# A gated feed-forward kernel: the transposition of the activations of batches 2 to 7 moves from TensorE to two transposing DMAs per batch

## The reference

```python
scale = cond @ norm_w.T + 1.0                       # (8, 512)
ms = mean(x * x, axis=-1)
h = x * (scale[:, None, :] * rsqrt(ms + 1e-6))
u = h @ up_w.T                                      # up_w: (4096, 512)
val, gate = split(u, 2, axis=-1)
h = val * gelu(gate)                                # exact gelu, 2048 wide
hq = round-to-int8-levels(h), one scale per token   # 127 / max|h|
wq = ternary(down_w), one scale for the matrix
out = hq @ wq.T + x
```

## Time and profile before

| what | value |
|---|---|
| median of the runs | 810.25 us |
| profiled execution: span from first to last instruction | 807.4 us |
| TensorE busy | 772.0 us (96%) |
| DVE busy | 605.6 us (75%) |
| ACT busy | 443.2 us (55%) |
| POOL busy | 255.6 us (32%) |
| DMA queue of SP | 152.06 MB, 55.5% of 16 engines |

### The profile page before, as it was taken

How to read it: one execution, slowest core, us unless ns; L and a number is a source line. 1 busy time by engine, 2 the same in 40 slices (tenths; PEclk the granted TensorE clock), 3 DMA queues, 4 the chain that set the end, 5 groups by cost and what they waited for, 6 DMA issues and landing times.

```text
span 807.4 us, 18034 instructions
## 1 busy us (share of the span) xinstructions
PE 772.0 (96%) x6401; PEld 635.0 (79%) x6401; DVE 605.6 (75%) x852; ACT 443.2 (55%) x1025; POOL 255.6 (32%) x318
## 2 busy tenths in 40 slices
PE   5898988999799999999999999999999999999998
PEld 4687877788688877897788877898788877888753
DVE  5987987799568973899558973898558973887367
ACT  5687767587566643555446643555446643554323
POOL 3875966354422321123212321122212321111021
PEclk9999999999999999999999999999999999999999
DMA  5485764876465554654565554654565545555432
GB/s 207 169 264 170 239 226 175 309 243 218 160 223 198 185 187 148 223 206 145 188 213 200 184 169 151 230 203 140 193 219 195 182 162 162 188 187 175 133 126 83
DMA packets 37963, 152.90 MB, mean 189 GB/s; under 512 B 3608, under 2 KB 4128, under 8 KB 37920
## 3 DMA queue, kind: packets, MB, share of 16 engines
q1 hardware_dynamic: 37376, 152.06, 55.5%
q10 hardware_dynamic: 544, 0.27, 0.1%
HBM read 130.16 MB, written 22.15 MB: 189 GB/s over the span
## 4 chain that ended last, share of the span: by engine, by line
PE 71%; DVE 7%; DMA 1%; issue 1%; ACT 1%; SPq 0%; DVEq 0%; ACTq 0%
PE Y L1142 11%; PE A L1091 11%; PE A L1094 11%; PE A L1093 11%; PE B L1091 8%; PE B L1094 8%; PE B L1093 8%; DVE h L872 2%; DMA wslots<-w_scratch 1%; DVE h L838 1%; PE X L1039 1%; DVE h L832 1%; DVE mpart L851 1%; PE X L1131 1%; DVE q L877 1%
## 5 line engine op out<-in xcount | busy, mean ns | idle before, releaser
L1091 PE MATMUL A<-xT,wslots 128*128 (+1 forms) x1024 | 280.9, 274 | 13.4 <-ACT snapC L616 9.1
L1093 PE MATMUL A<-xT,wslots 128*128 (+1 forms) x1024 | 280.9, 274 | 0.0
L1094 PE MATMUL A<-xT,wslots 128*128 (+1 forms) x1024 | 280.9, 274 | 0.0
L509 POOL TENSOR_TENSOR snapC<-snapC 128x256 f32<-128x256 f32 x128 | 100.5, 785 | 503.4 <-ACT snapC L616 503.3
L1091 PE MATMUL B<-xT,wslots 128*128 (+1 forms) x768 | 210.4, 274 | 2.1 <-DVE h L832 2.1
L1093 PE MATMUL B<-xT,wslots 128*128 (+1 forms) x768 | 210.3, 274 | 0.0
L1094 PE MATMUL B<-xT,wslots 128*128 (+1 forms) x768 | 210.2, 274 | 0.0
L838 DVE SCALAR_TENSOR_TENSOR h<-h,c_all,g 128x512 f32<-128x512 f32 (+1 forms) x128 | 103.7, 810 | 111.0 <-ACT g L639 110.7
L1091 PEld LDWEIGHTS A<-xT,wslots 128*128 128x128 f16 x1024 | 100.7, 98 | 30.3 <-ACT snapC L616 11.0
L1093 PEld LDWEIGHTS A<-xT,wslots 128*128 128x128 f16 x1024 | 100.7, 98 | 14.6
L1094 PEld LDWEIGHTS A<-xT,wslots 128*128 128x128 f16 x1024 | 100.8, 98 | 12.2
(11 more groups left out here) (137 smaller groups left out, 944.0 us busy)
## 6 DMA issues: line engine op xcount, KB each, us to landing
wslots<-w_scratch SPq DMA_DIRECT2D x105, 896.0 KB, 4.6
w_scratch<-wslots SPq DMA_DIRECT2D x15, 896.0 KB, 5.2
wst<-in_L_cond_up_w_dram SPq DMA_DIRECT2D x16, 512.0 KB, 6.5
xin<-in_x_dram SPq DMA_DIRECT2D x8, 1024.0 KB, 7.5
dwb<-in_L_cond_down_w_dram SPq DMA_DIRECT2D x16, 512.0 KB, 4.4
wst<-in_x_dram SPq DMA_DIRECT2D x28, 256.0 KB, 5.3
out_dram<-wst SPq DMA_DIRECT2D x28, 256.0 KB, 2.1
xin<-in_x_dram SPq DMA_DIRECT2D x4, 256.0 KB, 4.1
```

What stands on the lines that cost most here:

```text
L509: pool.tensor_tensor(snapC[:, s % 2, 0:H], snapC[:, s % 2, 0:H], snapC[:, s % 2, H:T], ALU.add)\
L1091: pe.matmul(into, high, xh, start=(start and kp == 0), stop=False, skip_group_check=not start)
L1093: pe.matmul(into, high, xl, start=False, stop=False, skip_group_check=not start)
L1094: mm = pe.matmul(into, low, xh, start=False, stop=last, skip_group_check=not start)
```

## The change

Only x of batches 2 to 7 is touched; batches 0 and 1 keep the old way. The work is done with the tokens on the partitions: DVE multiplies each tile of xin by the token's factor and the channels' scale in one instruction (`normalise_scaled`, two tiles in step 5, two in step 6); for that the scales of all batches are turned once in batch 0 (one transpose, one ACT copy), stored to `scl_rows`, and one row is loaded per batch as a broadcast (`load_scl`). POOL mixes blocks of xin in steps 7 and 10, ACT writes the high parts of one depth pair to a staging buffer `xstage` (in xf's room) in steps 7, 8, 11, 12, DVE the low parts in steps 8, 9, 12, 13, now after `value(s)`. SP then turns the staging buffer, high and low parts together (3584 float16 columns, 128 partitions), into xT by one transposing DMA per depth pair (`turn_x`): the first is issued after the weights of slot 13, the second after those of slot 15, each after a wait of SP for its low parts. ACT's high part of the second pair waits for the first DMA to have landed; TensorE waits for both at the start of the next batch. The 16 transposes of TensorE and the four copies `x_out` of each of these batches go.

```diff
-    RMS_AT, REFINE_AT, NORMALISE_AT = 4, 5, 5
-    XT_AT = {6: 0, 7: 1, 8: 2, 11: 3}
-    XF_AT = {6: 0, 7: 1, 10: 2, 11: 3}
-    XMIX_AT = {8: 0, 12: 1}
-    XHI_AT = {8: 0, 9: 1, 12: 2, 13: 3}
-    XLO_AT = {9: 0, 10: 1, 13: 2, 14: 3}
+    RMS_AT, REFINE_AT = 4, 5
+    NORMALISE_AT = {5: (0, 1), 6: (2, 3)}
+    XMIX_AT = {7: 0, 10: 1}
+    XHI_AT = {7: 0, 8: 1, 11: 2, 12: 3}
+    XLO_AT = {8: 0, 9: 1, 12: 2, 13: 3}
+    XTURN_AFTER = {13: 0, 15: 1}
...
+            def load_scl(b):
+                row = scl_rows[b:b + 1] if isinstance(b, int) else scl_rows[bass.ds(b, 1)]
+                sp.dma_start(scl_b[:, :], row.to_broadcast([P, D])).then_inc(scl_b_loaded, 16)
+
+            def turn_x(b, kp):
+                sp.wait_ge(xlo_ready, 4 * b + (2 * kp + 2))
+                sp.dma_start_transpose(x_turned(b, kp), xstage[:, :, :].rearrange("p a n -> p (a n)"))\
+                  .then_inc(x_turned_in[kp], 16)
...
                 for s in range(5, 15):
                     load_slot(b, s)
+                    if not final and s in XTURN_AFTER:
+                        turn_x(b + 1, XTURN_AFTER[s])
...
                 load_slot(b, 15)
                 if not final:
+                    turn_x(b + 1, XTURN_AFTER[15])
                     load_slot(b + 1, 4)
...
+                    sp.wait_ge(scl_copied, 1)
+                    sp.dma_start(scl_rows.rearrange("b (k p) -> k b p", p=P),
+                                 scl_kb[:, :]).then_inc(scl_stored, 16)
             sp.wait_ge(w_stored[ring_of(3)], 16 * LOADS[ring_of(3)])
+            sp.wait_ge(scl_stored, 16)
+            load_scl(2)
             batch(1, first=True)
...
+            def x_high_stage(b, kp, cut):
+                act.wait_ge(xmix_steps, 8 * b + (4 * kp + (4 if cut else 2)))
+                if cut == 0:
+                    if kp:
+                        act.wait_ge(x_turned_in[0], 16 * (b - 1))
+                    act.activation(xstage[:, 0, 0:4 * H].rearrange("p (h t n) -> p h t n", h=2, n=P), xn_blocks(kp),
+                                   ACT.Copy).then_inc(xhi_ready, 1)
...
+            def normalise_scaled(b, tiles):
+                dve.wait_ge(rstd_ready, b + 1)
+                dve.wait_ge(scl_b_loaded, 16 * (b - 1))
+                for t in tiles:
+                    dve.scalar_tensor_tensor(out=xin[:, t, :], in0=xin[:, t, :], scalar=rstd[:, t:t + 1],
+                                             in1=scl_b[:, :], op0=ALU.mult, op1=ALU.mult).then_inc(xn_ready, 1)
...
-                            normalise(b + 1)
-                        if s in XLO_AT:
-                            x_low(b + 1, *divmod(XLO_AT[s], 2), XLO_AT[s] + 1)
+                        if s in NORMALISE_AT:
+                            normalise_scaled(b + 1, NORMALISE_AT[s])
...
                     value(b, s)
+                    if not final and s in XLO_AT:
+                        x_low_stage(b + 1, *divmod(XLO_AT[s], 2), XLO_AT[s] + 1)
                     largest(of, before)
...
             def batch(b, first=False, final=False):
-                pe.wait_ge(xlo_ready, 4 * b + 4)
+                if first:
+                    pe.wait_ge(xlo_ready, 4 * b + 4)
+                else:
+                    for kp in range(KP):
+                        pe.wait_ge(x_turned_in[kp], 16 * (b - 1))
...
                     p6(b, s)
-                    if not final and s in XT_AT:
-                        transpose_x(b + 1, XT_AT[s])
```

More of the change, by code:

```diff
@@ L120, in gated_ffn_program @@
     SLOT = 2 * NA * KP * P
+    scl_rows = nc.dram_tensor("scl_rows", (B, D), F32, kind="Internal").ap()
     scratch = nc.dram_tensor("w_scratch", (FT - KEPT, P, SLOT), F16, kind="Internal").ap()
@@ L152, in gated_ffn_program @@
         xf1 = sb("xf", [P, NB * H], F32)
+        xsum = sb("xsum", [P, (NB - 4) * H], F32)
+        scl_b = sb("scl_b", [P, D], F32)
+        scl_kb = sb("scl_kb", [KT * B, P], F32)
         ident = sb("ident", [P, P], F32)
@@ L177, in gated_ffn_program @@
         squared = xf1[:, 0:TT * D // 2].bitcast(F16).rearrange("p (t d) -> p t d", d=D)
+        xstage = xf1[:, :].bitcast(F16).rearrange("p (a n) -> p a n", a=2)
         q32 = q[:, :].bitcast(F32)
@@ L229, in x_part, with x_turned, xn_block, xn_blocks @@
         def x_part(b, part, kp, blk, n):
-            at = b % 2 * (2 * KP * NB * H) + ((part * KP + kp) * NB + blk) * H
+            at = b % 2 * (2 * KP * NB * H) + ((kp * 2 + part) * NB + blk) * H
             return xT[:, bass.ds(at, n * H)]
+        def x_turned(b, kp):
+            at = b % 2 * (2 * KP * NB * H) + kp * 2 * NB * H
+            return xT[:, bass.ds(at, 2 * NB * H)].rearrange("p (j r) -> p j r", r=P)
+        def xn_block(kp, k_half, t_half):
+            k = k_half * KP + kp
+            return xin[:, t_half * KP:(t_half + 1) * KP, k * P:(k + 1) * P]
+        def xn_blocks(kp):
+            return xin[:, :, :].rearrange("p t (h n) -> p h t n", h=2)[:, :, :, kp * P:(kp + 1) * P]
+        def x_sum(i):
+            return xsum[:, i * H:(i + 1) * H].rearrange("p (t n) -> p t n", t=2)
         def xf_of(b, kp):
@@ L288, in gated_ffn_program @@
         xlo_ready = sem("xlo_ready")
+        scl_turned = sem("scl_turned")
+        scl_copied = sem("scl_copied")
+        scl_stored = sem("scl_stored")
+        scl_b_loaded = sem("scl_b_loaded")
+        x_turned_in = [sem(f"x_turned_in{i}") for i in range(KP)]
         w_loaded = [sem(f"w_loaded{i}") for i in range(WSTAGE)]
@@ L389, in batch @@
                 if not final and not first:
-                    sp.wait_ge(xT_psum, KT * b + KT)
+                    sp.wait_ge(xlo_ready, 4 * b + 4)
                     load_x(b + 1)
+                    load_scl(b + 1)
                 if first:
@@ L452, in _ @@
             batch(LAST, final=True)
-            sp.wait_ge(xT_psum, KT * B)
+            sp.wait_ge(xlo_ready, 4 * B)
             load_x(LAST)
@@ L512, in x_mix, with x_mix_second @@
             def x_mix(b, kp):
+                done = 8 * b + 4 * kp
+                if kp == 0:
+                    pool.wait_ge(xn_ready, TT * b + 2)
+                else:
+                    pool.wait_ge(xlo_ready, 4 * b + 2)
+                b12, b21, b22 = xn_block(kp, 0, 1), xn_block(kp, 1, 0), xn_block(kp, 1, 1)
+                pool.tensor_tensor(x_sum(T3 - T2), b22, b12, ALU.subtract).then_inc(xmix_steps, 1)
+                pool.tensor_tensor(b12, b12, xn_block(kp, 0, 0), ALU.subtract).then_inc(xmix_steps, 1)
+                pool.wait_ge(xmix_steps, done + 2)
+                pool.tensor_tensor(x_sum(0), b22, b12, ALU.subtract).then_inc(xmix_steps, 1)
+                pool.wait_ge(xmix_steps, done + 3)
+                pool.tensor_tensor(x_sum(T4 - T2), b21, x_sum(0), ALU.subtract).then_inc(xmix_steps, 1)
+            def x_mix_second(b, kp):
                 f = xf_of(b, kp).rearrange("p (a t) -> p a t", a=NB)
@@ L552, in _ @@
                 if s in XMIX_AT_0:
-                    x_mix(1, XMIX_AT_0[s])
+                    x_mix_second(1, XMIX_AT_0[s])
                 if s + 2 < FT:
@@ L575, in squares @@
                     act.wait_ge(xlo_ready, 4 * b)
+                    if not isinstance(b, int) or b > 2:
+                        act.wait_ge(x_turned_in[KP - 1], 16 * (b - 2))
                 for t in tiles:
@@ L597, in x_high @@
                     .then_inc(xhi_ready, 1)
+            def x_high_stage(b, kp, cut):
[5 more added lines that the diff above has]
+                                   ACT.Copy).then_inc(xhi_ready, 1)
+                else:
+                    act.activation(xstage[:, 0, 4 * H:NB * H], xsum[:, :], ACT.Copy).then_inc(xhi_ready, 1)
             def w_high(p, c):
@@ L667, in normalise, with x_ahead, x_second_ahead @@
                     act.activation(xin[:, t, :], xin[:, t, :], ACT.Copy, scale=rstd[:, t:t + 1]).then_inc(xn_ready, 1)
[L669 to L675, removed]
+            def x_ahead(b, s):
+                if s in SQUARES_AT:
+                    squares(b, SQUARES_AT[s])
+                if s in XHI_AT:
+                    x_high_stage(b, *divmod(XHI_AT[s], 2))
+            def x_second_ahead(s):
+                if s in SQUARES_AT_0:
+                    squares(1, SQUARES_AT_0[s])
+                if s in XF_AT_0:
+                    x_out(1, XF_AT_0[s])
+                if s in XHI_AT_0:
+                    x_high(1, *divmod(XHI_AT_0[s], 2))
+                if s == FT - 2:
+                    act.wait_ge(scl_turned, 1)
+                    act.activation(scl_kb[:, :], X[0:KT * B, 0:P], ACT.Copy).then_inc(scl_copied, 1)
             def batch(b, first=False, final=False):
@@ L730, in _ @@
                     normalise(1)
-                x_ahead(1, s, SQUARES_AT_0, XF_AT_0, XHI_AT_0)
+                x_second_ahead(s)
                 if s in DW_SUM:
@@ L773, in normalise @@
                 dve.wait_ge(rstd_ready, b + 1)
-                for t in range(2 if is_first(b) else TT):
+                for t in range(2):
```

(20 more changed lines are left out.)

## The result

The changed kernel is slower: 818.32 us in the median of four runs (817.76 to 819.72) beside 810.18 us of the kernel before; the ratio is 1.0108, with a 95% interval of 1.0089 to 1.0128. The direction was forecast, the size was not: +8.1 us where +3.8 stood. The profiled execution took 819.72 us, the slowest of the four, with a span of 817.9.

What follows compares the result with a forecast made beforehand. TensorE was taken as the bound, with DVE as long from step 4 to p5(9). At D = 7, 3.25 + 0.3 + 0.5 = +4.05 took the span from 807.4 to 811.45; with 2.85 more, 814 us, range 803 to 838.

Steps and rivals of the forecast that it cites:

- What bounds the kernel: TensorE bounds most of a looped batch, but from step 4 to p5(9) DVE is as long as it.
- the three groups: TensorE's transpose groups in steps 6, 7, 8, 0.44 us each: removing them is worth nothing, as DVE sets p5(9).
- DVE's list up to `value(7)`: Steps 5 and 6: four multiplications take 2.68 us instead of 1.59, so `value(7)` ends 1.09 us later, at 370.00.
- The stand: TensorE's wait before p5(9), which could come at 367.17 but starts near 370.05, held by DVE's `value(7)`.
- My best case: POOL's first mix, moved to step 7, hides behind DVE's maximum: 0.5 or 1.4 us back; the faster rival's chance was 0.23.
- The net per looped batch: Batches 2 to 6: 1.09 us of DVE's delay less 0.44 of TensorE's saving, +0.65 each, +3.25 in all.
- the 0.44 of step 11: TensorE leads from step 9 on, so removing the transpose group of step 11 gives 0.44 us per looped batch.
- the prediction's own formula: Added us: 3.25 + 0.3 + (D - 6.5) + 5 x (D - 7.0 where above) + (D - 7.2 where above).
- D: Time of a transposing DMA from issue to landing: 7 us assumed, bounds 4.6 and 11.9; the much-slower rival had chance 0.20.
- Room for D: First transposing DMA, looped batch: up to 7.0 us is free before ACT's step 11 work; beyond, us for us.
- Batch 1: DVE's delay 0.9, transposes -0.44, ACT wait -4.4, first transposing DMA D - 2.6: together D - 6.5 us.
- The rest (batch 0): Batch 0's transpose, small ACT copy, 16 KB store and SP's wait for it: 0.3 us, at worst 1.5.

Runs made afterwards that it cites:

- two-operand run: The changed kernel with the old two-operand multiplication for x, the channels' scale left out: 796.18 us (ratio 0.9824).
- late turn: The changed kernel with two unread 896 KB device-memory copies issued right ahead of the first transposing DMA, so it lands later: 844.78 us.
- narrow mix: The changed kernel with POOL's mix of the first depth pair cut from 128 to 16 columns of each block: 815.0 us.

## Why the prediction was right in its direction and wrong in its size

- **What bounds the kernel.** Right. TensorE's list was the longer only outside steps 4 to 9, and the three groups within were worth little: 1.8 of 6 us when cut alone, while the change as a whole lost.
- **DVE's list up to `value(7)`.** The stand was forecast at 370.05 - 367.17 = 2.9 and was 2.5 to 2.7. The multiplications cost 0.67 each as taken. From the first of them to the end of `value(7)` DVE took 19.97 us in batch 3 beside 19.06 before, so 0.9 more where 1.09 was forecast. The slowing by POOL was taken as the same in the new place and was 1.7 after 1.9. That it nearly agreed is luck: which instructions it hits hangs on tenths of a microsecond, and in the two-operand run 1.7 of it went and 0.6 came elsewhere. My best case, 1.4 back, is not reached in balance.
- **The net per looped batch, +0.65.** This is the step that failed. "The stretch is 1.09 longer" is all the step charges for the stand. Without the clock the net was +0.33: 0.9 of DVE's delay, less the 0.44 of step 11, less 0.17 in step 1, which the sum doesn't have and whose cause I did not follow. The stand's second price, 1.4 to 1.6 us of half clock in four of five looped batches and 2.8 in batch 1, is missing from the sum. With the stand filled by idle transposes 5.6 us went, more than the 4.1 by which the forecast was short. The trace of before held a warning: behind the 4.4 of the earlier trace rows it has 12 matmuls 0.21 apart, and from 203 to 213 us its mean clock is 0.83 (the last three numbers are clock, DMA share and GB/s).

```profile
203.00:213.00 10.00, 5.59 (x43) 4.44 (x42) 5.58 (x7) 4.32 (x10) 2.87 (x3) 0.83 0.43 143
```

With the clock kept up the changed kernel takes 812.7, and the prediction's own formula gives 813.4 for D = 6.1. That these agree so well is partly luck, for the formula has 3.25 for the looped batches, where 1.6 was measured without the clock.

- **D.** The forecast takes 7, my estimate between the bounds 4.6 and 11.9; no run shows a 7. The runs showed 6.1 in the loop (6.9 at most), beside 4.6 for a slot load of the same bytes, and 8.3 and 7.9 in batch 1. While the first turn of batch 3 is under way (384.2 to 390.4 us), 3632 of the queue's 3721 packets are under 512 bytes and the DMA share is 0.99. How much of the 1.5 us over a slot load is due to the small packets was not separated. The prediction's range names D = 10.9 for its end at 838; its own sum gives 838 at D = 10.4.
- **Room for D.** Put at 7.0 and measured at 7.1 in the two batches of the late turn whose clock stayed up; never reached in the loop of the changed kernel. The us-for-us price beyond is as forecast.
- **Batch 1.** Forecast D - 6.5, so +1.8 at its D of 8.3. Measured from the copy of p1(1) of batch 1 to that of batch 2 (88.69 before, 89.99 after) +1.3, but not by the terms of the forecast. TensorE waited 3.2 for DVE at p5(9) where it had waited 0.7, so 2.5 more where 0.9 was forecast. The half clock behind that cost 2.8, where before it cost 1.2. TensorE was so late by then that it waited for ACT only 2.3, where D - 2.6 is 5.7. The second turn cost 0.8. The number is near by luck.
- **The rest (batch 0).** 0.3 assumed. The profiled execution lost 1.5 up to step 1 of batch 1, but its clock was 0.68 from 20 to 40 us, where the kernel before had 1.00. The run with the narrow mix, which has the change's batch 0 and also a clock of 1.00 there, gets to step 1 of batch 1 at 150.49, the kernel before at 150.41. So most of the 1.5 goes with the clock of that stretch, and the profiled execution of the kernel before with the maximum regrouped has such a stretch too (0.71 from 20 to 40 us).

## What to carry to other kernels

A saved instruction on the busiest engine is worth what the next engine's list lets through between two points where they meet. Find the last gap ahead of each wait and sum the other engine's list from there. In this kernel a stand of TensorE of 2.5 us was followed by some 1.5 us lost to the clock in four of five looped batches, so the change cost more than the stand, and idle work in the gap was cheaper than none (812.7 beside 818.32 us). Before trading engines, move what the late engine does to those that have gaps; here the trade, which cost 8 us as it was made, gained 14 once that was done and the maximum was regrouped.

## What was not expected of the hardware

- The granted clock fell to half (0.50 from 374.3 to 377.4 us of the changed kernel) behind stands of 2.2 to 2.5 us at p5(9) in most looped batches (four of five in the changed kernel, four of five with the narrow mix, three of five with the late turn) and in none behind stands of 0.9 to 1.1 us, and cost 1.4 to 1.6 us each time. In the late turn's batches 4 to 6 it did not fall behind waits of 2.9 to 3.1 us for ACT. So the length of the stand alone does not decide it, and what does stays open here.
- Beside POOL's two-input operations DVE's `SCALAR_TENSOR_TENSOR` (0.75 to 1.21), its two-operand `TENSOR_SCALAR` (0.43 to 0.83) and the `TENSOR_TENSOR` that ends the maximum (0.69 to 1.25) were slowed, the `TENSOR_REDUCE` of the maximum was not (3.76 and 3.78 beside the mix or part of it, 3.74 ahead of it). A shift of DVE by 1.1 us removed 1.7 us of it and added 0.6.
- Turning 896 KB, in packets of 256 bytes, took 6.1 us in the median of the loop and held SP's sequencer for 4.1 to 4.9 us; in the median a slot load of the same size held it for 0.32.
